# Moving the small arithmetic of four norms from VectorE to GpSimd and ScalarE

## The reference

```python
ln_out = layernorm(hidden_states, ln1_s, ln1_b); ... x = hidden_states + attn_out     # "self"
ln_out = layernorm(x, ln2_s, ln2_b);             ... x = x + cross_out                # "cross"
ln_out = layernorm(x, ln3_s, ln3_b)
x = x + gelu(ln_out @ w1 + b1) @ w2 + b2                                              # "mlp0"
...
attn_out = attn_out @ out_w + out_b + residual                                        # "lat"
out = rmsnorm(attn_out, postnorm_w)
out = gelu(out @ mlp_w1 + mlp_b1) @ mlp_w2 + mlp_b2 + residual                        # "mlp1"
```

## Time and profile before

| | |
|---|---|
| three runs | 1088.24, 1089.6, 1089.82 us, median 1089.6 |
| profiled execution | span 1086.8 us from the first to the last instruction; the page gives no time around it |
| granted TensorE clock, mean | 0.983 of full |
| TensorE | 1004.1 us busy (92%) |
| VectorE | 988.4 us (91%), 2328 instructions |
| ScalarE | 849.4 us (78%), 1905 instructions |
| GpSimd | 681.9 us (63%), 909 instructions |
| chain that ended last | TensorE 37%, ScalarE 26%, VectorE 20%, issue 11%, GpSimd 4%, DMA 2% |

### The profile page before, as it was taken

The page is one execution under the profiler, slowest core; times in us unless marked ns, Lnnn a source line. Parts: engine busy times, 40 slices in busy tenths (PEclk is TensorE's granted clock), DMA queues, the critical chain, the costliest instruction groups (busy, mean ns, idle before and its releaser), DMA issues.

```text
span 1086.8 us, 46478 instructions
## 1 busy us (share of the span) xinstructions
PE 1004.1 (92%) x19180; PEld 890.8 (82%) x19180; DVE 988.4 (91%) x2328; ACT 849.4 (78%) x1905; POOL 681.9 (63%) x909
## 2 busy tenths in 40 slices
PE   6776989999999999999999999999999999998997
PEld 5665778888888888888888888888888888886786
DVE  4989897999999999999999999999999999988763
ACT  3446789887888888888788888878888888786894
POOL 3777575666666667666667676666676676655221
PEclk9879999999999999999999999999999999999999
DMA  8843112222322222222222222222222222311111
GB/s 275 280 114 74 42 39 41 44 45 58 59 49 51 52 57 43 49 54 58 58 49 45 57 47 48 50 58 58 49 49 54 56 44 49 61 37 37 31 37 36
DMA packets 169700, 67.70 MB, mean 62 GB/s; under 512 B 151184, under 2 KB 167312, under 8 KB 168464
## 3 DMA queue, kind: packets, MB, share of 16 engines
q1 hardware_dynamic: 169488, 64.72, 26.1%
HBM read 26.93 MB, written 4.19 MB: 29 GB/s over the span
## 4 chain that ended last, share of the span: by engine, by line
PE 37%; ACT 26%; DVE 20%; issue 11%; POOL 4%; DMA 2%; SPq 0%; ACTq 0%; POOLq 0%; DVEq 0%
PE psum L457 9%; PE psum L598 7%; PE psum L630 7%; ACT staging L2017 7%; PE psum L470 6%; ACT hid_mlp L2017 6%; PE psum L564 3%; ACT L2003 3%; PE psum L584 3%; DVE mx_lat L1248 3%; ACT L2017 2%; ACT probT_self L2003 2%; DVE late L1267 2%; DVE mx_ctx L1254 2%; DMA turned_mlp<-pair_mlp 1%
## 5 line engine op out<-in xcount | busy, mean ns | idle before, releaser
L2499 POOL TENSOR_TENSOR prob_self<-prob_self,add_self 128x512 f32<-128x512 f32 x64 | 86.8, 1376 | 66.1 <-DVE prob_self L1238 63.4
L2499 POOL TENSOR_TENSOR prob_cross<-prob_cross,add_cross 128x512 f32<-128x512 f32 x64 | 94.5, 1495 | 52.9 <-DVE prob_cross L1238 52.9
L2505 POOL TENSOR_TENSOR late<-late,mx_ctx 128x512 f32<-128x512 f32 x64 | 67.3, 1053 | 86.6 <-DVE mx_ctx L1254 84.1
L2017 ACT ACTIVATE hid_mlp<-psum,folded,undo_in 128x128 f32<-128x128 f32 x256 | 95.6, 455 | 6.9 <-PE psum L457 6.4
L2017 ACT ACTIVATE staging<-psum,cols,undo_in 128x128 f32<-128x128 f32 x256 | 97.4, 481 | 3.3 <-PE psum L457 3.1
L457 PE MATMUL psum<-turned_mlp,hi_n 128*128 128x128 f16 x1024 | 94.2, 221 | 1.6 <-DVE late L1267 1.0
L630 PE MATMUL psum<-hi_n,staging 128*128 128x256 f16 x512 | 94.3, 273 | 1.5 <-DVE staging L1297 1.5
L457 PE MATMUL psum<-turned_mlp,hi_m 128*128 128x128 f16 x1024 | 93.4, 220 | 0.6 <-DMA turned_mlp<-pair_mlp 0.5
L630 PE MATMUL psum<-hi_m,parts_mlp 128*128 128x256 f16 x512 | 89.9, 273 | 1.2 <-DVE xb L1291 0.9
L457 PE MATMUL psum<-turned_mlp,lo_n 128*128 128x128 f16 x512 | 90.3, 221 | 0.0
L457 PE MATMUL psum<-turned_mlp,lo_m 128*128 128x128 f16 x512 | 89.6, 220 | 0.0
(11 more groups left out here) (265 smaller groups left out, 3850.0 us busy)
## 6 DMA issues: line engine op xcount, KB each, us to landing
xin<-in_x SPq DMA_DIRECT2D x32, 128.0 KB, 2.2
late<-in_ctxT SPq DMA_DIRECT2D x4, 1024.0 KB, 5.7
ctxT<-in_ctxT SPq DMA_DIRECT2D x32, 128.0 KB, 2.0
late<-in_x SPq DMA_DIRECT2D x4, 1024.0 KB, 5.6
out<-xb SPq DMA_DIRECT2D x32, 128.0 KB, 1.9
staging<-in_w_m SPq DMA_DIRECT2D x2, 1024.0 KB, 7.2
staging<-in_w_n SPq DMA_DIRECT2D x2, 1024.0 KB, 5.2
mask<-in_mask_cross SPq DMA_DIRECT2D x32, 32.0 KB, 2.0
```

The costliest lines, as they stand in the source:

```text
L2017: last = e.activation(hid[t][g][:, j * P:(j + 1) * P], ps[:, j * P:(j + 1) * P], ACT.Gelu_apprx_tanh, bias=b1[:, 4 * g + j:4 * g + j + 1], ...
L2499: e.tensor_tensor(ch, ch, over_heads(a[:, :]), ALU.add).then_inc(sem["added_" + t], 1)
L2505: e.tensor_tensor(ch, ch, over_keys(max_of("ctx", h)), ALU.subtract).then_inc(sem["shifted_ctx"], 1)
```

## The change

VectorE's `moments` keeps bn_stats and bn_aggr for self, cross and mlp0, and is no longer called for mlp1. GpSimd's `root` makes `var` itself from `mv` (or from `mean_square`) with a tensor_scalar, then the power, then `shift` with a tensor_scalar from the mean and `rstd`. For mlp1 ScalarE makes `mean_square` with a Square activation that sums along the row (`squared_rows`). In the loop it is ScalarE's first call of a round; in head and drain it stands ahead of each `scaled_high`, in places further ahead. All other calls keep their places. The scaling of the context on GpSimd gets a second multiplication, by 1.0. Counts of semaphores follow. `bn_mlp1`, `mv_mlp1`, the `minus_mean` tiles and `shift_mlp1` are gone, and a tile `squared` of 128x256 is new.

```diff
@@ VectorE
             def moments(u, t):
-                src, shrink = residual(t, u), 2.0 ** (-2 * XHAT_UP)
-                steps, n = sem["moments_" + t], 4 * u
+                src, steps, n = residual(t, u), sem["moments_" + t], 2 * u
+                q.wait_ge("moments_" + t, n)
...
                 e.bn_stats(bn[t][:, :], src[:, :]).then_inc(steps, 1)
                 q.wait_ge("moments_" + t, n + 1)
+                q.wait_ge("rstd_" + t, 3 * u)
                 e.bn_aggr(mv[t][:, :], bn[t][:, :]).then_inc(steps, 1)
-                q.wait_ge("moments_" + t, n + 2)
-                if t == "mlp1":
-                    e.scalar_tensor_tensor(mean_square[:, :], mv[t][:, 0:1], mv[t][:, 0:1], mv[t][:, 1:2],
-                                           ALU.mult, ALU.add).then_inc(steps, 1)
-                    q.wait_ge("moments_" + t, n + 3)
-                    e.tensor_scalar(var[t][:, :], mean_square[:, :], L1_EPS, shrink, ALU.add, ALU.mult).then_inc(steps, 1)
-                else:
-                    q.wait_ge("rstd_" + t, 2 * u)
-                    e.tensor_scalar(minus_mean[t][:, :], mv[t][:, 0:1], -1.0, None, ALU.mult).then_inc(steps, 1)
-                    e.tensor_scalar(var[t][:, :], mv[t][:, 1:2], L0_EPS, shrink, ALU.add, ALU.mult).then_inc(steps, 1)
...
             for t in range(FILL, SLOTS):
                 q_bias_self(t - 2)
-                moments(t - 7, "mlp1")
                 k_spread(t - 2, "self", 0)
@@ ScalarE
             def normalize(u, t):
                 q.wait_ge("x_lo_" + t, u)
-                q.wait_ge("rstd_" + t, 2 * u + 2)
+                q.wait_ge("rstd_" + t, 3 * u + 3)
...
+            def squared_rows(u):
+
+                q.wait_ge("x_lat", u + 1)
+                q.wait_ge("rstd_mlp1", 2 * u)
+                e.activation(squared[:, :], residual("mlp1", u)[:, :], ACT.Square, scale=1 / ROOT_H,
+                             accum_out=mean_square[:, :]).then_inc(sem["mean_square_mlp1"], 1)
...
             for t in range(FILL, SLOTS):
+                squared_rows(t - 7)
                 values(t - 2, "self")
                 exponential(t - 6, "lat", 0)
@@ GpSimd
-                e.tensor_scalar(ctxT[i][:, :, :], ctxT[i][:, :, :], up_of("ctx"), None, ALU.mult).then_inc(sem["ctx_halves"], 1)
+                e.tensor_scalar(ctxT[i][:, :, :], ctxT[i][:, :, :], up_of("ctx"), 1.0, ALU.mult, op1=ALU.mult).then_inc(sem["ctx_halves"], 1)
...
             def root(u, t):
                 q.wait_ge("constants", MINUS_HALF)
-                q.wait_ge("moments_" + t, 4 * u + 4)
-                q.wait_ge("x_lo_mlp1" if t == "mlp1" else "xn_" + t, u)
-                e.tensor_tensor(rstd[t][:, :], var[t][:, :], minus_half[:, :], ALU.pow).then_inc(sem["rstd_" + t], 1)
+                shrink, done = 2.0 ** (-2 * XHAT_UP), sem["rstd_" + t]
+                if t == "mlp1":
+                    q.wait_ge("mean_square_mlp1", u + 1)
+                    q.wait_ge("x_lo_mlp1", u)
+                    n, src, eps = 2 * u, mean_square[:, :], L1_EPS
+                else:
+                    q.wait_ge("moments_" + t, 2 * u + 2)
+                    q.wait_ge("xn_" + t, u)
+                    n, src, eps = 3 * u, mv[t][:, 1:2], L0_EPS
+                e.tensor_scalar(var[t][:, :], src, eps, shrink, ALU.add, op1=ALU.mult).then_inc(done, 1)
+                q.wait_ge("rstd_" + t, n + 1)
+                e.tensor_tensor(rstd[t][:, :], var[t][:, :], minus_half[:, :], ALU.pow).then_inc(done, 1)
                 if t != "mlp1":
-                    q.wait_ge("rstd_" + t, 2 * u + 1)
-                    e.tensor_tensor(shift[t][:, :], minus_mean[t][:, :], rstd[t][:, :], ALU.mult).then_inc(sem["rstd_" + t], 1)
+                    q.wait_ge("rstd_" + t, n + 2)
+                    e.tensor_scalar(shift[t][:, :], mv[t][:, 0:1], rstd[t][:, 0:1], -1.0, ALU.mult, op1=ALU.mult).then_inc(done, 1)
```

More of the change, by code:

```diff
@@ L133 @@
 moments_mlp0 rstd_mlp0 xn_mlp0 x_hi_mlp0 x_lo_mlp0 across_mlp0
-moments_mlp1 rstd_mlp1 x_hi_mlp1 x_lo_mlp1 across_mlp1
+mean_square_mlp1 rstd_mlp1 x_hi_mlp1 x_lo_mlp1 across_mlp1
 qk_mm_self q_self k_self v_mm_self val_self q_mm_cross q_cross
@@ L275, in build @@
         part = {t: [a[:, :].bitcast(F16) for a in parts[t]] for t in parts}
-        bn = {t: sb("bn_" + t, [P, 6]) for t in NORMED}
-        mv = {t: sb("mv_" + t, [P, 2]) for t in NORMED}
+        bn = {t: sb("bn_" + t, [P, 6]) for t in NORMED[0:3]}
+        mv = {t: sb("mv_" + t, [P, 2]) for t in NORMED[0:3]}
         var = {t: sb("var_" + t, [P, 1]) for t in NORMED}
         rstd = {t: sb("rstd_" + t, [P, 1]) for t in NORMED}
-        minus_mean = {t: sb("minus_mean_" + t, [P, 1]) for t in NORMED}
-        shift = {t: sb("shift_" + t, [P, 1]) for t in NORMED}
+        shift = {t: sb("shift_" + t, [P, 1]) for t in NORMED[0:3]}
         mean_square = sb("mean_square", [P, 1])
+        squared = sb("squared", [P, H])
         mx = {t: sb("mx_" + t, [P, NH]) for t in SETS}
@@ L1163, in moments @@
                 else:
-                    q.wait_ge({"cross": "x_self", "mlp0": "x_cross", "mlp1": "x_lat"}[t], u + 1)
+                    q.wait_ge({"cross": "x_self", "mlp0": "x_cross"}[t], u + 1)
                 e.bn_stats(bn[t][:, :], src[:, :]).then_inc(steps, 1)
                 q.wait_ge("moments_" + t, n + 1)
+                q.wait_ge("rstd_" + t, 3 * u)
                 e.bn_aggr(mv[t][:, :], bn[t][:, :]).then_inc(steps, 1)
-                q.wait_ge("moments_" + t, n + 2)
-                if t == "mlp1":
-                    e.scalar_tensor_tensor(mean_square[:, :], mv[t][:, 0:1], mv[t][:, 0:1], mv[t][:, 1:2],
-                                           ALU.mult, ALU.add).then_inc(steps, 1)
-                    q.wait_ge("moments_" + t, n + 3)
-                    e.tensor_scalar(var[t][:, :], mean_square[:, :], L1_EPS, shrink, ALU.add, ALU.mult).then_inc(steps, 1)
-                else:
-                    q.wait_ge("rstd_" + t, 2 * u)
-                    e.tensor_scalar(minus_mean[t][:, :], mv[t][:, 0:1], -1.0, None, ALU.mult).then_inc(steps, 1)
-                    e.tensor_scalar(var[t][:, :], mv[t][:, 1:2], L0_EPS, shrink, ALU.add, ALU.mult).then_inc(steps, 1)
             @of_unit
@@ L1531, in _ @@
             add_residual(0, "lat")
-            moments(0, "mlp1")
             low_pair(3, "mlp0")
@@ L1637, in _ @@
             q_bias_self(UNITS - 2)
-            moments(UNITS - 7, "mlp1")
             hidden_lo(UNITS - 8, "mlp1", 0)
@@ L1754, in _ @@
             low_pair(UNITS - 1, "cross")
-            moments(UNITS - 5, "mlp1")
             hidden_lo(UNITS - 6, "mlp1", 0)
@@ L1795, in _ @@
             low_pair(UNITS - 1, "mlp0")
-            moments(UNITS - 4, "mlp1")
             denominators(UNITS - 3, "lat")
@@ L1820, in _ @@
             lat_low(UNITS - 1)
-            moments(UNITS - 3, "mlp1")
             add_mlp(UNITS - 5, "mlp1")
@@ L1849, in _ @@
             add_residual(UNITS - 1, "lat")
-            moments(UNITS - 1, "mlp1")
             add_mlp(UNITS - 4, "mlp1")
@@ L1941, in scaled_high @@
             @of_unit
+            def squared_rows(u):
[3 more added lines that the diff above has]
+                             accum_out=mean_square[:, :]).then_inc(sem["mean_square_mlp1"], 1)
+            @of_unit
             def scaled_high(u):
                 q.wait_ge("across_mlp1", 16 * u)
-                q.wait_ge("rstd_mlp1", u + 1)
+                q.wait_ge("rstd_mlp1", 2 * u + 2)
                 e.activation(pair["mlp1"][:, 0, :], residual("mlp1", u)[:, :], ACT.Copy, scale=rstd["mlp1"][:, 0:1]).then_inc(sem["x_hi_mlp1"], 1)
@@ L2127, in _ @@
             values(1, "ctx")
+            squared_rows(0)
             scaled_high(0)
@@ L2191, in _ @@
             exponential(UNITS - 6, "ctx", 1)
+            squared_rows(UNITS - 7)
             scaled_high(UNITS - 7)
@@ L2210, in _ @@
             heads_high(UNITS - 2, "self")
+            squared_rows(UNITS - 6)
             scaled_high(UNITS - 6)
@@ L2248, in _ @@
             normalize(UNITS - 2, "mlp0")
+            squared_rows(UNITS - 5)
             scaled_high(UNITS - 5)
@@ L2273, in _ @@
             hidden_hi(UNITS - 5, "mlp1", 1)
+            squared_rows(UNITS - 4)
             scaled_high(UNITS - 4)
@@ L2284, in _ @@
             exponential(UNITS - 2, "ctx", 0)
+            squared_rows(UNITS - 3)
             scaled_high(UNITS - 3)
@@ L2301, in _ @@
             hidden_hi(UNITS - 3, "mlp1", 0)
+            squared_rows(UNITS - 2)
             scaled_high(UNITS - 2)
@@ L2305, in _ @@
             hidden_hi(UNITS - 3, "mlp1", 1)
+            squared_rows(UNITS - 1)
             scaled_high(UNITS - 1)
```

2 lines of the change are left out of this document (removed).

## The result

The kernel became slower. The median is 1119.4 us (four runs, 1117.29 to 1124.98) against 1089.7 for the kernel before in the same job, a ratio of 1.0279 with a 95% interval of 1.0254 to 1.0304. The forecast was 1101.5 us, its range ended at 1110. So the sign was right and the size was not: 12 us were forecast and 30 came.

A forecast was written before the change was run, and what follows sets the result against it. A chain of waits through TensorE, ScalarE and VectorE, not busy time, was taken to bound the kernel. 10.1 + 1.4 + 0.4 = 11.9 us on 1089.6 gave 1101.5 us, chance 0.62, range 1087 to 1110 (its own 1095 to 1107).

The forecast's parts named there:

- What bounds the kernel: Loop: a chain of waits over TensorE, ScalarE and VectorE, 30.78 us a round, with a second path nearly as long.
- Part 1, VectorE's relief at zero: Loop: VectorE drops 1.88 us a round, 60 us over 32 units, before existing waits; gain 0, bound 1.0 a round.
- the prediction's signs: Listed observations that would show it right, among them VectorE busy 60 us less and rounds of 31.2 to 31.3 us.
- Rival A: VectorE's busy time is the bound: 1065.6 us in full, chance 0.07; 1086 in a partial form, chance 0.07.
- Part 2, the square at 0.42 us a round: Loop: ScalarE's square delays the late exponentials 1.18 us, stalling TensorE at bank 4; 24 rounds, 10.1 us.
- rival D: The square reloads ScalarE's table, two loads of 1.28 us each round: 62 us more, 1151, chance 0.01.
- Part 3, GpSimd's path: Loop: added GpSimd instructions lengthen the second path 0.5 us, mostly covered; 0.06 a round left, 1.4 us.
- Part 3, the ctx scaling at zero: GpSimd's context scaling with a second operation may shrink or grow, but nobody waits for ctxT in the loop; cost 0.
- Rival B: VectorE's port lock holds the first MLP's power on GpSimd: 0.8 us a round, 1109.2 us, chance 0.15.
- Part 4, the drain at +0.4 us: Head and drain: head 0, +-3; drain +0.6 for the square, less 0.2 for shorter work; sum +0.4 us.
- Time outside the span: The median lay 2.8 us above the profiled span; this difference was carried over unchanged.
- The lock: VectorE and GpSimd share ports exclusively; a two-input VectorE operation can hold GpSimd, 549 ns powers becoming 987.

The follow-up runs named there:

- scalar_alone_mended: scalar_alone with the square behind val_self in the loop and five of seven drain squares moved ahead: 1093.0 us, 1.0015 of the kernel before.
- mlp0_on_vector: Kernel after with square behind val_self, five drain squares ahead, one-operation context scaling, first MLP's minus_mean and var back on VectorE: 1095.4 us, 1.0052 of before.
- gpsimd_without_self: gpsimd_alone with minus_mean and var of the norm of self back on VectorE: 1111.6 us, 1.0194 of the kernel before.
- scalar_alone: Kernel before with only the second MLP's mean square moved to ScalarE, its scaling and power on GpSimd: 1112.3 us, 1.0199 of the kernel before.
- ctx_one_op: Kernel after with the context's scaling as a single multiplication again: 1118.1 us, 1.0257 of the kernel before.
- square_after_values: Kernel after with squared_rows and the values call for self exchanged in ScalarE's loop: 1127.6 us, 1.0320 of the kernel before.
- before_bias_last: Kernel before with GpSimd's plus_bias of the second MLP moved behind both subtractions of ctx: 1076.5 us, 0.9881 of the kernel before.
- the mended kernels: Versions with the square behind val_self in the loop and five drain squares moved ahead: 1088.7 to 1095.4 us.
- mended_bias_last: mlp0_on_vector with GpSimd's plus_bias of the second MLP moved behind both subtractions of ctx: 1088.7 us, 0.9991 of the kernel before.
- gpsimd_alone: Kernel before with only the three layer norms' scaled variances and shifts moved to GpSimd: 1109.2 us, 1.0168 of the kernel before.

## Why the prediction was wrong

**What bounds the kernel: right.** Two roads through a round, nearly as long, of which the busy shares tell nothing. What was missing is the list of TensorE's claims along the second, and the drain.

**Part 1, VectorE's relief at zero: right.** The instructions taken out had 60 us, as worked out, but the busy time fell by 33 only, where the prediction's signs name 60: pair_self grew by 8.8 us in all and prob_self's subtraction by 9.8, both held by GpSimd, and some of the short ones had lain beside their neighbours. Nevertheless scalar_alone_mended and mlp0_on_vector keep the round at 30.79. The instructions removed stand before waits. Rival A is out. The zero holds for these kernels and not everywhere: with xn_mlp late, the pair of self costs 0.15 us a round (gpsimd_without_self).

**Part 2, the square at 0.42 us a round: right in mechanism, too small by 0.11.** ScalarE idles 0.87 us before it (forecast 0.85). The third exponential is 1.2 us late (1.18). But the slack at bank 4 was taken as 0.76 us with 0.06 from the exponential's end to the projection, and where TensorE does wait there the rows have 0.14 (3.31 to 3.45 after x_lat, medians of scalar_alone). So TensorE is delayed 0.55 and not 0.42, inside the bounds of 0.32 to 0.67, and scalar_alone's round is +0.53. That TensorE's wait at line 470 is put down as 0.39 looks nearer to the forecast than it is. A square took 0.42 and its read 0.19, and val_self could start 0.54 us after the square did; I had taken 0.50. The kernels before and after both have 72 table loads; rival D is out.

**Part 3, GpSimd's path: its sum was right, its cause was not.** xn_mlp moved by 0.64 us, beyond the 0.56 that was the bound. By the rows of one round this is 0.18 in cross, where var_cross is held at 0.60 but the power behind it no longer is (553 ns in the median instead of 987), 0.27 for the first MLP's var (0.31 forecast), and 0.19 for small delays before and behind it, which were not in the sum. The prediction let 0.42 of the delay be covered by the square's stall and left 0.06. The cover holds and is whole: ctx_one_op has both parts, the same median round as scalar_alone, and a loop 11.8 us longer than before, where 10.1 + 1.4 = 11.5 were forecast. That the sum fits so well is partly luck: the square alone has 10.8. But the road was another: not the DMA and the hidden layer, but val_ctx behind xn_mlp on ScalarE, and the bank that TensorE claims of it. Without the square this part costs 0.53 us a round by itself, which the prediction doesn't say and which shows again in square_after_values.

**Part 3, the ctx scaling at zero: this step failed.** The range for its duration was fair (0.45 us less at the median). "Nobody waits for ctxT" is true and not enough: what stands behind it on GpSimd moved onto pair_self, on a VectorE that had 0.25 us of slack before and none after. 725.6 - 721.2 = 4.4 us in the loop, where the same edit in the kernel before costs 0.9 (710.3 - 709.4). With it the loop is 16.2 us longer, where 11.5 were forecast. Rival B named the lock, but at another instruction; that its 0.8 us a round came near the 0.75 measured is chance.

**Part 4, the drain at +0.4 us: this step failed by the most.** It measured +13.5. The error is in "+0.6, less 0.2": I priced one square on one stretch of the chain. There are seven, each directly ahead of the scaled_high that needs it, and the chain of the drain runs through those powers and scaled_highs. The square's part alone makes the drain 11.4 us longer (scalar_alone), and moving five away takes back 8.5 of it (scalar_alone_mended), or 5.7 in the kernel after. So where the squares stand is the larger part of it, shown. Seven times 0.5 + 1.09 us, the square and the wait behind it, would be 11 us too, but that is not how it adds up: counted from the drain's start, the seven scaled_highs of scalar_alone are 1.6, 4.5, 8.5, 10.4, 13.4, 12.7 and 12.8 us later than before. The last two squares cost nothing, because those scaled_highs waited 2.0 and 2.6 us for the old statistics, and the second to fifth cost up to 4 us each; what lengthens them beyond 1.6 us isn't settled. GpSimd's part adds 4.2 alone. The head at 0 +-3 was right (+1.7), though it counted 18 norms up to 210 us, where GpSimd has 22 powers, and the number shows little: in the profiled executions it lies between 213.7 and 220.8 us, with a granted clock of 0.91 of full before, 0.88 after and 0.83 in scalar_alone and before_bias_last between 80 and 120 us. I leave what belongs to the kernels in it open.

**Time outside the span.** I carried over 2.8 us. The profiled execution of the kernel after took 1119.96 us, 1.8 above its span. This is no part of the error.

**The lock.** What the Trainium skill states in SBUF — State Buffer, section "SBUF: two separate sides", that VectorE and GpSimd hold their shared ports against each other, agrees with mx_ctx here: it ended 0.01 us after GpSimd's addition, took 0.68 us, and 0.15 without it. The prediction used the rule only one way, VectorE holding GpSimd. The cases on the path, mx_ctx and pair_self, were the other way round.

The forecast missed by 17.9 us in the medians and by 19.5 in the spans of the profiled executions. Of the 19.5, the drain has 13.1, the loop 4.7 (the ctx scaling alone 4.4) and the head 1.7.

Open: the 1.4 to 3.4 us that remain in the drain of the mended kernels, and the head.

## What to carry to other kernels

Don't price a relief by busy time: follow each removed instruction to the next wait on its engine, and start from zero if there is one. Price an added instruction with everything queued behind it in order, up to each bank or buffer that somebody claims, and count it again in the drain, once for every unit: a producer set right before its consumer on the same engine makes that engine stand through the round trip (here 0.5 + 1.09 us), less what the consumer waited before. A price holds for one kernel: the square that cost nothing in scalar_alone_mended has TensorE 0.23 us late in each round once another hold is gone. And an expectation whose numbers all come true can still have the wrong cause, so look where in the order of time the delay first shows. And look for short instructions that take several times their shortest duration on the chain: the exchange of two calls on another engine gave 1.2%, the whole move of work less than nothing.

## What the runs showed of the hardware

- On GpSimd the tensor_scalar of 128x256 f32 on ctxT with two multiplications takes 479 to 481 ns at its shortest, with one 922 to 932.
- VectorE operations with two SBUF inputs that start while a GpSimd addition runs took longer, the smallest too: 128x8 in 0.68 us instead of 0.15, 128x256 in 0.95 instead of 0.62 (0.36 at the shortest), 128x512 in 1.12 instead of 0.69.
- A Square of 128x256 f32 with a sum along the row takes ScalarE 0.42 us, plus 0.19 for the read of the accumulator, of which the next instruction sees 0.54 in all. It needs no table load of its own: the count of loads is 72 with the 32 squares and without them, and 29 squares ran behind the load for exponentials, 3 behind that for gelu.
- Where TensorE waits for a PSUM bank that ScalarE or VectorE reads out, its product starts 0.14 to 0.15 us after the end of that reading (bank 4 in scalar_alone and mended_bias_last, bank 1 in gpsimd_alone, bank 4 in gpsimd_without_self).
- Small GpSimd instructions of 128x1: 0.19 us for a tensor_scalar, 0.55 for a power, 0.60 for the tensor_scalar where it is held.
